# The first of an image's four additions made by a DMA that adds, issued by GpSimd

## The reference

```
avg = g.mean(axis=(2, 3))
wk  = sigmoid(avg @ w1.T + b1).reshape(b * c, 1, 3, 3)      # one 3x3 kernel per image and channel
y   = conv(g, wk, padding 1, one group per image and channel) + conv_bias
out = x + (g - y) * fscale * g + y
```

## Time and profile before

| | us |
|---|---|
| median of three runs | 263.33 (262.99 to 266.01) |
| span of the profiled execution, first to last instruction | 260.2 |
| busy: PE, DVE, POOL, ACT | 241.6, 232.6, 225.0, 210.6 |
| POOL's 63 additions | 165.5 |
| one image in the middle, by the pattern of the rows | 14.44 |

### The profile page before, as it was taken

The page is one execution under the profiler, slowest core; times in us unless marked ns, Lnnn a source line. Parts: engine busy times, 40 slices in busy tenths (PEclk is TensorE's granted clock), DMA queues, the critical chain, the costliest instruction groups (busy, mean ns, idle before and its releaser), DMA issues.

```text
span 260.2 us, 9778 instructions
## 1 busy us (share of the span) xinstructions
PE 241.6 (93%) x3906; PEld 189.5 (73%) x3906; DVE 232.6 (89%) x558; ACT 210.6 (81%) x388; POOL 225.0 (86%) x254
## 2 busy tenths in 40 slices
PE   4899989899899999999999999999999999999991
PEld 3577657658687887878787877878787878888770
DVE  3899999799999999999999999999999998746555
ACT  2177998797988989897989989898979989899510
POOL 1331889599999999999999999999999999999982
PEclk9999999999999999999999999999999999999999
DMA  7999931993989989798979799897989742444476
GB/s 252 414 428 422 412 130 72 339 395 122 341 326 362 345 319 374 264 390 300 347 326 362 292 345 383 295 375 273 362 333 355 296 204 118 184 184 184 185 302 245
DMA packets 10990, 77.75 MB, mean 299 GB/s; under 512 B 1344, under 2 KB 1472, under 8 KB 3264
## 3 DMA queue, kind: packets, MB, share of 16 engines
q1 hardware_dynamic: 10944, 77.12, 77.7%
HBM read 39.37 MB, written 37.75 MB: 296 GB/s over the span
## 4 chain that ended last, share of the span: by engine, by line
PE 56%; DVE 25%; issue 11%; POOL 3%; DMA 2%; ACT 1%; SPq 0%; DVEq 0%; ACTq 0%; POOLq 0%
PE conv_ps L433 36%; PE conv_ps L439 12%; DVE outs L614 10%; DVE pieces L542 9%; DVE taps L559 4%; PE dyn_ps L417 3%; PE dyn_ps L425 2%; DMA xs<-x 2%; POOL outs L893 1%; PE conv_ps L497 1%; DVE taps L566 1%; DVE row_stats L548 1%; POOL inv_std L862 1%; ACT xs L735 1%; DVE outs L624 1%
## 5 line engine op out<-in xcount | busy, mean ns | idle before, releaser
L433 PE MATMUL conv_ps<-xs,taps 64*64 64x448 f32 x1536 | 219.9, 547 | 5.6 <-DVE outs L614 5.2
L893 POOL TENSOR_TENSOR outs<-outs,linear 128x1152 f32<-128x1152 f32 x63 | 165.5, 2645 | 1.3 <-DVE outs L614 1.2
L614 DVE SCALAR_TENSOR_TENSOR outs<-xs,beta,conv_ps 128x576 f32<-128x576 f32 x128 | 102.8, 804 | 18.5 <-PE conv_ps L433 18.2
L433 PEld LDWEIGHTS conv_ps<-xs,taps 64*64 64x64 f32 x1536 | 101.4, 132 | 24.3 <-issue 13.0
L439 PE MATMUL conv_ps<-xs,taps 64*64 64x128 f32 x1536 | 114.0, 271 | 0.0
L771 ACT ACTIVATE linear<-xs,slope 128x576 f32<-128x576 f32 x128 | 109.1, 856 | 2.9 <-POOL outs L893 2.9
L542 DVE BATCH_NORM_STATS2 pieces<-xs 128x6 f32<-128x64 f32 (+1 forms) x256 | 102.6, 448 | 4.8 <-DMA xs<-x 4.8
L439 PEld LDWEIGHTS conv_ps<-xs,taps 64*64 64x64 f32 x1536 | 93.5, 132 | 8.7 <-issue 2.6
L735 ACT ACTIVATE xs<-xs,shift 128x594 f32<-128x594 f32 x128 | 99.5, 780 | 0.0
L862 POOL TENSOR_TENSOR inv_std<-numbers,minus_half 128x8 f32<-128x8 f32 x16 | 26.4, 1648 | 4.3 <-ACT dev_mean L741 4.3
L559 DVE TENSOR_TENSOR taps<-dyn_ps,tap 128x1512 f32<-128x1512 f32 (+1 forms) x19 | 27.8, 1473 | 0.0
(11 more groups left out here) (67 smaller groups left out, 143.1 us busy)
## 6 DMA issues: line engine op xcount, KB each, us to landing
xs<-x SPq DMA_DIRECT2D x30, 1188.0 KB, 11.2
out<-outs SPq DMA_DIRECT2D x30, 1152.0 KB, 5.2
xs<-x SPq DMA_DIRECT2D x8, 297.0 KB, 4.9
out<-outs SPq DMA_DIRECT2D x3, 576.0 KB, 3.4
out<-outs SPq DMA_DIRECT2D x2, 288.0 KB, 2.6
cst<-const SPq DMA_DIRECT2D x1, 275.5 KB, 5.3
w1s<-w1r SPq DMA_DIRECT2D x1, 144.0 KB, 5.1
gates<-gate SPq DMA_DIRECT2D x1, 8.0 KB, 5.6
```

The source lines that it names most:

```text
L433: return nc.tensor.matmul(tile(i, g, taken)[:, START:BANK], taps[given, i % 2, at:at + HALF], xs[given, i % XBUFS, g, 0:PAIRED, 1 + shift: ...
L614: nc.vector.scalar_tensor_tensor(out=outs[:, i % OBUFS, g].rearrange("p (k w) -> p k w", w=COLS), in0=xs[:, i % XBUFS, g, :, 1:1 + COLS], ...
L893: nc.gpsimd.tensor_tensor(tile, tile, linear[:, PAIR * k:PAIR * (k + 1)].rearrange("p g n -> p (g n)"), ALU.add).then_inc(out_ready, 1)
```

## The change

Pair 0 of every image, the last one too, is no longer added by a POOL instruction. POOL waits for the same products and linear parts, issues a DMA whose source is `linear` and whose destination is `outs`, both in SBUF, with addition as the accumulating operation, and goes on. The DMA's end is counted on a semaphore of its own for each `outs` buffer (`dma_added`). Who waited on `out_ready` for pair 0 (SP's store and ACT's linear part) now waits on `dma_added`, and the count of `out_ready` is by three pairs an image. Pairs 1 to 3 stay on POOL.

```diff
+BY_DMA = 0
 ...
+        dma_added = [sem(f"dma_added{b}") for b in range(OBUFS)]
 ...
+        def wait_for_pair(eng, i, k):
+            if k == BY_DMA:
+                eng.wait_ge(dma_added[i % OBUFS], 16 * (i // OBUFS + 1))
+            else:
+                eng.wait_ge(out_ready, (PAIRS - 1) * i + k + (k < BY_DMA))
 ...
                 for h in range(STORES):
-                    sp.wait_ge(out_ready, PAIRS * i + per * (h + 1))
+                    for k in range(per * h, per * (h + 1)):
+                        wait_for_pair(sp, i, k)
                     store(i, h * per * PAIR, per * PAIR)
 ...
             for k in range(PAIRS - 1):
-                sp.wait_ge(out_ready, PAIRS * (B - 1) + k + 1)
+                wait_for_pair(sp, B - 1, k)
                 store(B - 1, k * PAIR, PAIR)
 ...
-                if g % PAIR == 0:
-                    at_least(act, out_ready, PAIRS * (i - 1) + g // PAIR + 1)
+                if g % PAIR == 0 and i > 0:
+                    wait_for_pair(act, i - 1, g // PAIR)
 ...
                 tile = outs[:, i % OBUFS, PAIR * k:PAIR * (k + 1)].rearrange("p g n -> p (g n)")
+                if k == BY_DMA:
+                    pool.dma_start(tile, linear[:, PAIR * k:PAIR * (k + 1)].rearrange("p g n -> p (g n)"),
+                                   accum_op=ALU.add).then_inc(dma_added[i % OBUFS], 16)
+                    return
                 nc.gpsimd.tensor_tensor(tile, tile, linear[:, PAIR * k:PAIR * (k + 1)].rearrange("p g n -> p (g n)"),
                                         ALU.add).then_inc(out_ready, 1)
```

## The result

The changed kernel takes 308.6 us (median of 4 runs, 308.28 to 310.27) against 263.16 us for the kernel before (4 runs, 262.0 to 266.01): a ratio of 1.171, with a 95% interval of 1.163 to 1.179. That is 45.4 us more. The ratios, here and in the experiments, are taken over fast runs alone and can differ by half a per cent from the quotient of the medians. The forecast was 271 us, in a range of 262.5 to 282.

A forecast was written before the change was run, and what follows sets the result against it. The prediction took PE and DVE, holding each other at 14.44 us an image, as the bound. A span of 260.2 us, 3.1 around it and 8 of lateness from the addition gave 271 us, range 262.5 to 282.

The forecast's parts named there:

- The gain of 0: On POOL, the removed additions, 2.65 us of each image, only become a longer wait for the mean: gain 0.
- Two passes: On the DMA engines, the addition reads two operands, taken as two passes at 433 GB/s: 2.7 us, bounds 1.4 and 4.3.
- The third of the added waits: ACT's first linear part of the next image waits for the landing: 1.2 us too late, 0.6 us an image.
- the threshold of 6.3 us: A landing later than 6.3 us after POOL's issue stops ACT, then PE, then the mean, then POOL.
- the engines' side of the sum: DMA engines busy 13.1 us plus 2.7 is 15.8 us an image, 1.4 over the period: 10.6 us after a 3.4 us cushion.
- hidden: Rival, chance 0.35: the addition costs little more than one pass and lands within 6.3 us; time 263.3 us.
- the engines as the bound: Rival, chance 0.19: two passes at slower rates make the DMA engines set the pace; 281 or 289 us.
- faster: Rival, chance 0.04: without POOL's addition beside them DVE's instructions run faster, 0.4 us an image; 258 us.
- The other two waits: SP's first store and DVE's products two images later also wait for the landing, at no cost.
- 7.5 us: The addition's time from POOL's issue to landing: 3.4 us plain DMA, 2.7 store packets, 1.4 second pass.
- The count of images: Loads and stores meet in images 2 to 11, so lateness was counted over ten images.
- Taking the middle of two readings: ACT's wait, 6 us, and the engines' excess, 10.6 us, were called the same lateness and put at 8 us.

The follow-up runs named there:

- e3: The changed kernel with pair 0 added by nobody, neither POOL nor a DMA, and without the waits on it: 265.14 us, ratio 1.002 to the kernel before.
- e1: The changed kernel with pair 0's linear parts in two buffers in turn, so ACT waits for the DMA of two images before: 274.31 us, ratio 1.043.
- e5: The changed kernel with SP holding an image's second store, and the loads behind it, until the next image's addition has landed: 307.98 us, ratio 1.160.
- e4: The changed kernel with eight spare matmuls on PE ahead of the dynamics of every second image: 298.6 us, ratio 1.132 to the kernel before.
- e2: The changed kernel with POOL's DMA copying the linear parts over the products, adding nothing: 283.56 us, ratio 1.075 to the kernel before.
- e7: The changed kernel with two buffers in turn for pair 0's linear parts and a plain copy in place of the adding DMA: 264.27 us, ratio 0.998.
- e6: The changed kernel with the DMA adding only the first 128 floats of each partition of group 0: 274.4 us, ratio 1.034 to the kernel before.

## Why the prediction was wrong, point by point

**The gain of 0 was right.** The 42 us of POOL's work were covered by the wait for the mean, in the middle, as the earlier trace rows had it; e3 shows it without any DMA.

**The issue was covered, right.** It takes 0.89 us, inside the bounds of 0.34 and 2.65, and in the turn shown POOL still waits 2.00 us behind it.

**Two passes, right in kind and a little too small.** The forecast took 2.7 us for two passes against 1.4 for one. An adding packet takes 365 ns against 181 for a plain one. In the kernel as it runs, the rows give (0.171 x 308.4) / 16 = 3.3 us of all engines for each addition, so it was dearer by 0.6, inside the upper bound of 4.3.

**Who waits, right.** The third of the added waits, ACT's first linear part, is the one that pays; the loop over two images holds, and the threshold of 6.3 us nearly: PE's 4.57 us of standing with a landing of 11.6 put it at 7.0. Two of the signs named for it came otherwise. ACT's long wait, 4.8 to 5.7 us from image 4 to image 12, comes in every second image and not once an image, with 1.3 us or less in those between. And the DMA share fell, where above 0.95 was expected; that sign belonged to the engines' side of the sum. Of the rivals, hidden fell with the landing, the engines as the bound came true only in e1, and faster fell with DVE's 805 ns.

**The other two waits cost nothing, right.** SP waits for the landing too, in its queue's own waits of the changed kernel:

```profile
SPq L327 <- DMA outs<-linear: 41.0, 13, 7.4
```

But DVE's waits for loads are 4.4 us in all, against 4.8 before, and no wait of DVE is for a store: what SP issues late is still early enough in a kernel that has become slower.

**The step that failed is the landing: "7.5 us".** It was added up as 3.4 us (a plain DMA on an almost empty queue), 2.7 (the store's packets) and 1.4 (the second pass), and left out SP's two loads behind the store: every packet of the addition stands in turn with one of theirs. It also took store and addition to share the engines from the start, where the addition had none until the store's packets were through. It measured 11.5 at the median. In the turn shown it is 3.9 us until the first packet, 7.0 of turns until the last one is through, and 0.7 to landing: 11.6. With a store and no loads it is 7.5 to 8.7 (e5's section), close to the forecast, so the loads are what was missing. Without company it is 5.4 to 6.0 (e5), so the base of 3.4 + 1.4 was also 0.6 to 1.2 too low. A row that warned of it was there: the load's 9.1 us in the earlier trace rows, for 1188 KB that are 2.8 us at 433 GB/s.

**The count of images was too low.** Ten images, in which loads and stores meet, were counted, five turns of the loop. ACT's wait acts beyond them: the trace has it in the seven even images 2 to 14, with 3.6, 5.0, 5.4, 5.7, 5.6, 4.8 and 2.0 us, the last of them without loads.

**The clock was not in the sum.** PE that stands in front of the dynamics then runs for 3.4 or 6.8 us at the 1.2 GHz level.

PE's own rows tell how the two parts divide. From DVE's first product of image 2 to that of image 14, first in the kernel before, then in the changed one, the windows and PE's wait in the second of them (before, PE has no such wait) are:

```profile
59.11:230.68 171.57, 166.64 (x2913) 135.91 (x2910) 165.19 (x395) 153.82 (x285) 167.57 (x181) 1.00 0.83 309
...
62.01:274.81 212.80, 182.45 (x2915) 148.33 (x2915) 166.23 (x396) 155.29 (x289) 146.41 (x181) 0.93 0.81 283
...
PE dyn_ps L426 <- ACT avg_rows L756: 25.7, 8, 4.8
```

These twelve images take 41.2 us more. PE stands for 25.7 us of it in front of the dynamics, and is busy for 15.8 us longer with the same matmuls, as 30.7 us at half the clock would have it (15.4): 41.5. So the wait is some 26 us and the clock some 16. That e4 gave back 8 to 10 and not more agrees with its 10.2 us that were left at the lower level. Of the 48.2 us between the two profiled spans, another 4.1 lie behind these images. The other 2.9 lie ahead of them and are not the change's: in e3, without any addition of pair 0, image 2's first product stands at 62.22 us too.

A small term was mis-sized as well: 3.1 us were taken for what lies around a span. The runs have 1.8 to 1.9 (310.27 us for a span of 308.4, 273.82 for 272.0 in e1).

**Taking the middle of two readings was wrong.** 6 us by ACT's wait and 10.6 by the engines were called the same lateness and joined to 8. They are two bounds, of which the later decides: e1 measures the engines' side alone at 9.8 us, near the 10.6. Its rate of 1.4 us an image is the forecast's; the count is not (seven images, after a longer cushion, for ten less 3.4 us), so the nearness of the totals is in part luck. In the change it is hidden behind the larger wait, with the engines at 0.84 of their time.

**The rule on a fit of a GpSimd DMA** did not hold here. Of an addition without company the trace shows 5.4 to 6.0 us, and with it 11.5. In the Trainium skill's page DMA: Bandwidth & Descriptors, Anatomy of one DMA, the fit for plain transfers gives an estimate of 3.35 us for these bytes; neither agrees, and the measurement decides. The plain copy of e2 is not that fast either: the soonest, image 0's, with a dozen packets of a load ahead of it, lands after 4.9 us.

**The rule that issuing engines share the 16 DMA engines** agrees. The packets of both queues take turns on them, and the share reaches 1.01 in e1. The same page of the Trainium skill, in Queues, rings and completion order, has each engine go round the queues that have work, packet by packet. Such turns show from 124.8 us on, with 103 packets to 94 in the stretch above; ahead of it, the trace has 126 packets of the store to none. What kept the addition back there stays open; the plain copy of e2 was kept back for less. In image 0, and in image 1 of e5, with no store and hardly a load beside it, its first packet comes some 1.5 us after the issue. No run here shows whether a packet of that page is one of the profile's.

## What to carry to other kernels

Before moving work off an engine, look at what that engine waits for next: if it is a result that comes at a fixed time, the freed time becomes waiting. A transfer's price for whoever waits on it is its landing in company, to be read from transfers that are under way in the same moment, not its bytes over a rate; then ask which instruction in an in-order queue stands behind that landing, and give it a second buffer if it comes too soon. A wait that PE gets out of this is dearer than its length, when the granted clock is lower after it: here 26 us of standing and 16 of slower matmuls.

## What the runs showed of the hardware

- A DMA that adds from SBUF onto SBUF holds a DMA engine for 365 ns a packet of 4,608 bytes at the median, a plain packet of the same size 181 ns (e2's copy, and SP's last stores). In two buffers, where only the operation differs, it is 10 us of 264 (e1 against e7).
- Behind a store issued in the same moment, the addition's first packet came 3.9 us after its issue, after 126 of the store's packets; a plain copy's after 2.8 to 3.2 (e2); with hardly anything beside it the addition's came after some 1.5 us. Then packets of the two queues alternated, whatever their size, and so 64 KB landed only after 7.7 us (e6).
- POOL needs 0.89 us to issue such a DMA, 0.64 for the plain copy of e2, SP 0.34 us for a store.
- In six images PE stood for 2.8 to 4.8 us in front of the dynamics; around the end of each of these waits the granted clock fell to 0.50 and stayed there for 3.4 or 6.8 us, nearly all of it with PE busy. Eight spare matmuls in front of the dynamics of every second image, which took some of these stretches away, made the kernel 10 us faster (e4).
